# Softmax scores of two head pairs per group, four places for transposed probabilities and an eleven-tile feed-forward in a two-phase attention kernel

## The reference

```python
def _layer(x, wqkv, qs, ksc, wo, lg, lb, w1, b1, w2, b2):
    h = shift_token(x)                       # DIM 256, 8 heads of 64
    q, k, v = jnp.split(h @ wqkv, 3, axis=-1)
    q = l2norm(q) * qs
    k = l2norm(k) * ksc
    q, k = rotary_xpos(q, k)
    o = local_attention(q, k, v)             # windows of 128, each sees itself and the one before
    x = x + o @ wo
    h = shift_token(x)
    h = (h - mu) / jnp.sqrt(var + 1e-05) * lg + lb
    a, g = jnp.split(h @ w1 + b1, 2, axis=-1)    # HID = 682 each
    h = a * jax.nn.gelu(g, approximate=False)
    return x + h @ w2 + b2
```

## Time and profile before

| | |
|---|---|
| median of 3 runs | 5799.47 us (5796.46 to 5799.69) |
| the profiled execution's own time | 5798.98 us |
| its span, first to last instruction | 5797.2 us |
| TensorE busy | 5642.3 us, 97% |
| VectorE, ScalarE, GpSimd busy | 4143.9, 3455.5, 960.7 us |
| mean granted TensorE clock | 0.993 of full speed |

### The profile page before, as it was taken

The page is one execution under the profiler, slowest core; times in us unless marked ns, Lnnn a source line. Parts: engine busy times, 40 slices in busy tenths (PEclk is TensorE's granted clock), DMA queues, the critical chain, the costliest instruction groups (busy, mean ns, idle before and its releaser), DMA issues.

```text
span 5797.2 us, 146068 instructions
## 1 busy us (share of the span) xinstructions
PE 5642.3 (97%) x57904; PEld 2646.8 (46%) x57904; DVE 4143.9 (71%) x10780; ACT 3455.5 (60%) x6979; POOL 960.7 (17%) x1905
## 2 busy tenths in 40 slices
PE   8999999999999999998999999999999999999998
PEld 3444444444444444443444444444444444444443
DVE  6887888788878878786666666666666666666664
ACT  4766666676666667665555555555555555555554
POOL 2222222222222222222000000000000101010100
PEclk9999999999999999999999999999999999999999
DMA  3333333333333333232100000000010000000000
GB/s 70 57 54 67 55 66 56 58 62 51 70 56 65 56 60 60 51 66 52 41 15 8 15 12 12 12 12 15 8 37 12 15 19 15 19 23 12 22 12 19
DMA packets 128424, 215.38 MB, mean 37 GB/s; under 512 B 39964, under 2 KB 40092, under 8 KB 126976
## 3 DMA queue, kind: packets, MB, share of 16 engines
q1 hardware_dynamic: 127744, 206.05, 17.6%
HBM read 45.48 MB, written 25.17 MB: 12 GB/s over the span
## 4 chain that ended last, share of the span: by engine, by line
PE 83%; issue 6%; ACT 6%; DVE 3%; POOL 2%; DMA 0%; POOLq 0%; ACTq 0%; SPq 0%; DVEq 0%
PE ps L564 22%; PE ps L693 14%; PE ps L814 12%; PE ps L996 6%; PE ps L1029 5%; PE ps L890 5%; PE ps L1016 5%; PE ps L898 4%; PE ps L915 4%; ACT pt L1247 3%; PE ps L937 2%; PE ps L866 1%; PE ps L875 1%; PE ps L948 1%; POOL pt L2054 1%
## 5 line engine op out<-in xcount | busy, mean ns | idle before, releaser
L1247 ACT ACTIVATE pt<-ps 128x1024 f32<-128x1024 f32 (+7 forms) x2048 | 1237.3, 653 | 621.4 <-PE ps L564 464.3
L693 PE MATMUL ps<-pt,va 128*32 128x512 f32 (+3 forms) x3072 | 1226.6, 487 | 19.9 <-POOL pt L2054 19.9
L693 PE MATMUL ps<-pt,ones 128*32 128x512 f32 (+3 forms) x6144 | 1236.4, 488 | 0.0
L693 PE MATMUL ps<-pt,vs 128*32 128x512 f32 (+3 forms) x3072 | 1230.1, 488 | 0.0
L1614 DVE CUSTOM_DVE_ANT_0 junk<-ps,causal 128x128 bf16<-128x128 f32 (+3 forms) x2048 | 977.9, 487 | 308.5 <-PE ps L564 292.3
L564 PE MATMUL ps<-kt,qt 96*32 96x512 bf16 (+3 forms) x12288 | 1016.6, 328 | 35.2 <-DVE mc L1614 16.3
L564 PE MATMUL ps<-qt,kt 98*32 98x512 bf16 (+3 forms) x12288 | 835.3, 328 | 22.2 <-ACT pt L1247 21.1
L1618 DVE TENSOR_REDUCE mc<-ps 128x1 f32<-128x512 f32 x1024 | 706.3, 690 | 157.6 <-PE ps L564 127.0
L2054 POOL TENSOR_SCALAR_AFFINE_SELECT pt<-pt 128x256 f32<-128x256 f32 x1024 | 469.5, 459 | 1938.2 <-ACT pt L1247 1936.7
L814 PE MATMUL ps<-wqkv,xs 128*128 128x512 f32 x1536 | 782.3, 619 | 0.0
L1364 ACT ACTIVATE sm<-sm,mxw 128x256 f32<-128x256 f32 (+1 forms) x1024 | 495.7, 485 | 339.4 <-DVE mxw L1783 339.0
(11 more groups left out here) (144 smaller groups left out, 8499.3 us busy)
## 6 DMA issues: line engine op xcount, KB each, us to landing
qt<-part SPq DMA_DIRECT2D x768, 64.0 KB, 2.4
kt<-part SPq DMA_DIRECT2D x768, 64.0 KB, 2.5
ya<-wy SPq DMA_DIRECT2D x128, 128.0 KB, 2.3
yb<-wy SPq DMA_DIRECT2D x128, 128.0 KB, 2.3
xs<-between_phases SPq DMA_DIRECT2D x32, 512.0 KB, 3.9
xt<-in_x SPq DMA_DIRECT2D x16, 512.0 KB, 5.9
between_phases<-z SPq DMA_DIRECT2D x16, 512.0 KB, 2.8
between_phases<-xo SPq DMA_DIRECT2D x16, 512.0 KB, 2.7
```

The source lines that it names most:

```text
L693: mmi = pe.matmul(ps[32 * q:32 * q + 32, 4 + half, lo - half * 512:hi - half * 512], w, probs(kb)[:, i, lo - first(kb):hi - first(kb)], st ...
L1247: act.activation(probs(kb)[:, i, kb * P - first(kb):1024 - first(kb)], ps[:, 2 * i:2 * i + 2, :].rearrange("p a q -> p (a q)")[:, kb * P:1 ...
```

## The change

It does four things.

1. Scores. The two head pairs 0 and 1 are issued one behind the other, and so are 2 and 3. The even pair uses columns 0 to 255 of banks 4 and 5, the odd pair columns 256 to 511. Only the even pair waits for `s_read`, and `largest` of either pair waits until both are made.
2. `ptw` has four places; the copy of pair `hp` waits for `weigh` of the same pair in the window before. In c = 0, 1 and 3 the four `weigh` of a window now stand together; in c = 2 they stand in three pieces.
3. The feed-forward uses tiles of 128 channels: five for the gate, five for the other half, and one of 106 rows of output that holds the last 42 channels of both (42 of the one, then 42 of the other from row 64 on). `hidden` has five tiles instead of six; `gated` of the sixth multiplies two tiles of SBUF, of 42 rows. `ffn_out` keeps 2 x 6 matmuls, the last with 42 rows.
4. The orders of the instructions on TensorE, ScalarE and VectorE are laid anew for each c. Some tiles change their addresses (`pt`, `cn`, `sqf`, `both`), and `fbank` alternates with m, since a half now has an odd number of uses of the two banks.

```diff
-HP = -(-HID // HB)
+HLAST = HID - (HB - 1) * P
+HPAIR = 64 + HLAST
-def fbank(use):
+def fbank(m, use):
-    return 2 if use % 2 else 7
+    return 2 if (m + use) % 2 else 7
+def score_cols(hp, n):
+    return slice(hp % 2 * 256, hp % 2 * 256 + n)
...
-        ptw = sb("ptw", [P, 2, 4, P], F32)
+        ptw = sb("ptw", [P, 4, 4, P], F32)
-        w1 = sb("w1", [P, 2, 2, HB, HP], F32)
-        w2 = sb("w2", [HP, HB, 256], F32)
+        w1 = sb("w1", [P, 2, 2 * HB - 1, P], F32)
+        w2 = sb("w2", [P, HB, 256], F32)
...
-                pe.wait_ge(s_read, done(W * 4 + hp))
+                if hp % 2 == 0:
+                    pe.wait_ge(s_read, done(W * 4 + hp))
                 n = P if W % WIN == 0 else 256
                 for q in range(2):
                     rows = slice(64 * q, 64 * q + 64)
-                    pe.matmul(ps[:, 4 + q, 0:n], qp[rows, hp, :],
+                    pe.matmul(ps[:, 4 + q, score_cols(hp, n)], qp[rows, hp, :],
...
-                    mmi = pe.matmul(ps[0:HP, fbank(6 + j), :], w1[:, kc, 1, j, :], cn[:, kc, :], start=kc == 0, stop=kc == 1)
+                    if j < HB - 1:
+                        mmi = pe.matmul(ps[:, fbank(m, 6 + j), :], w1[:, kc, j, :], cn[:, kc, :], start=kc == 0, stop=kc == 1)
+                    else:
+                        mmi = pe.matmul(ps[0:HPAIR, fbank(m, 6 + j), :], w1[:, kc, 2 * HB - 2, 0:HPAIR], cn[:, kc, :],
+                                        start=kc == 0, stop=kc == 1)
...
-                act.wait_ge(o_full, done(W * 4 + hp - 1))
+                act.wait_ge(o_full, done(W * 4 + hp - 3))
...
-                dve.wait_ge(s_full, done((W * 4 + hp) * 2 + 2))
+                dve.wait_ge(s_full, done((W * 4 + (hp | 1)) * 2 + 2))
...
+                else:
+                    dve.tensor_tensor(hh[0:HLAST, j, :], gb_[0:HLAST, j, :], glast[:, :], ALU.mult).then_inc(hh_done, 1)
```

More of the change, by code:

```diff
@@ L947, in mean @@
                 pe.wait_ge(xsum_done, done(m + 1))
-                pe.matmul(ps[:, fbank(3), :], mean_w[:], both[:, 0, :], start=True, stop=True).then_inc(fm_full, 1)
+                pe.matmul(ps[:, fbank(m, 3), :], mean_w[:], both[:, 0, :], start=True, stop=True).then_inc(fm_full, 1)
             def variance(m):
@@ L955, in variance @@
                 pe.wait_ge(ssum_done, done(m + 1))
-                pe.matmul(ps[:, fbank(4), :], mean_w[:], both[:, 1, :], start=True, stop=True).then_inc(fv_full, 1)
+                pe.matmul(ps[:, fbank(m, 4), :], mean_w[:], both[:, 1, :], start=True, stop=True).then_inc(fv_full, 1)
             def final_mean(m, W):
@@ L1015, in hidden @@
                 for kc in kcs:
-                    mmi = pe.matmul(ps[0:HP, fbank(13 + j), :], w1[:, kc, 0, j, :], cn[:, kc, :], start=kc == 0, stop=kc == 1)
+                    mmi = pe.matmul(ps[:, fbank(m, 13 + j), :], w1[:, kc, HB - 1 + j, :], cn[:, kc, :], start=kc == 0, stop=kc == 1)
                 if kcs[-1] == 1:
@@ L1065, in attend @@
                     scores(W + 1, 0)
+                    scores(W + 1, 1)
                 elif c == 1:
@@ L1073, in attend @@
                     transpose_p(W, 0)
+                    values(W, 0)
+                    final_mean(m - 1, W)
                     scores(W, 2)
+                    scores(W, 3)
+                    transpose_p(W, 1)
+                    values(W, 1)
+                    gate(m, 0, True, (0,))
+                    gate(m, 0, True, (1,))
+                    gate(m, 1, True, (0,))
+                    gate(m, 1, True, (1,))
+                    gate(m, 2, True, (0,))
+                    transpose_p(W, 2)
+                    gate(m, 2, True, (1,))
+                    gate(m, 3, True, (0,))
+                    gate(m, 3, True, (1,))
+                    transpose_p(W, 3)
+                    gate(m, 4, True, (0,))
+                    weigh(W, 0)
+                    weigh(W, 1)
+                    weigh(W, 2)
+                    weigh(W, 3)
+                    transpose_q(W + 1)
+                    gate(m, 4, True, (1,))
+                    gate(m, 5, True, (0,))
+                    transpose_k(W + 1)
+                    gate(m, 5, True, (1,))
+                    scores(W + 1, 0)
+                    scores(W + 1, 1)
+                elif c == 2:
+                    queries(W + 1, 0)
+                    queries(W + 1, 1)
+                    keys(W + 1, 0)
+                    keys(W + 1, 1)
+                    final_variance(m - 1, W)
+                    transpose_p(W, 0)
                     values(W, 0)
@@ L1077, in attend @@
                     transpose_p(W, 1)
-                    final_mean(m - 1, W)
+                    scores(W, 2)
                     scores(W, 3)
[L1080 to L1106, removed]
-                    values(W, 0)
-                    transpose_p(W, 0)
-                    values(W, 1)
-                    final_variance(m - 1, W)
-                    scores(W, 2)
                     hidden(m, 0, True, (0,))
@@ L1175, in _ @@
             scores(0, 0)
+            scores(0, 1)
             for W in range(LAST):
@@ L1186, in _ @@
                 gate(m, j, False)
-            for j in range(HB):
+            for j in range(HB - 1):
                 hidden(m, j, False)
```

230 lines of the change are left out of this document (122 added, 108 removed).

## The result

The changed kernel takes 5648.9 us (median of 4 runs, 5647.3 to 5651.5) against 5799.0 us before: a ratio of 0.974, 95% interval 0.973 to 0.976. The forecast was 5677, with a range from 5642 to 5734. The time fell by 150 us where 122 were forecast.

A forecast was written before the change was run, and what follows sets the result against it. TensorE's list of matmuls was taken to bound the second phase. Savings of 54.9 + 51 + 22 + 22 less 28 us of new waits gave 122 us, so 5799.0 became 5677 us, range 5642 to 5734.

The forecast's parts named there:

- What bounds the kernel: Second phase, 32 periods: as long as TensorE's list of matmuls takes to stream; the first phase costed at nothing.
- Eleven tiles: Feed-forward: each of the 32 halves loses one tile of two matmuls, 54.9 us off TensorE's list, nothing added.
- Scores in groups: Scores on TensorE: 256 fewer groups at 0.19 us each, plus 2.8 us for shared ways in, together 51 us less.
- the two bounds: Time of a group's second pair of scores: 0.43 us or 0.63 + 0.20; the term would be 103 or 0 us.
- `weigh` in larger pieces: Pieces of `weigh` on TensorE fall from 256 to 192, which with what follows them saves 22 us.
- Old and new waits: TensorE: old waits of `mean` and `hidden` go, 22 us less; new waits, mostly in c = 2, add 28 us.
- waits over bank 3: Three places in c = 2 where TensorE waits on transpose and copy: 0.27, 0.27 and 0.08 us a period.
- the third: Wait in c = 2 from `transpose_q` to `transpose_k`, 1.35 us of the 1.43 needed: 0.08 us late.
- Transpose 2 of c = 2: TensorE there waits for ScalarE's copy of pair 1: 16.6 us against 16.5, called level, with 0.05 us allowed.
- the groups do not merge: Rival: the second pair of a group drains the array like a lone one, 49 us lost, 5726 us; chance 0.06.
- The softmax chain: Rival: exponentials and copies behind long blocks bound some windows, 1 to 2 us a period more, 5709 to 5741; chance 0.15.
- The slower case: Rival: ScalarE's lateness at transpose 2 of c = 2 outlasts the period; at 5 us a period 5837 us; chance 0.03.

## Why the prediction was right, and where it was off

*What bounds the kernel* was right: the span followed TensorE's list of matmuls. The first phase did not move; the second phase's first projection starts at 2710.7 us in one trace and 2710.5 in the other.

*Eleven tiles*, 54.9 us: right as a length of the list, and wrong as a cost of nothing added. "The other tiles have 128 channels for 114, and stream the same 512 columns" was looked at for the tiles that grew, and not for the one that shrank to 42 rows: it costs 19 us by the medians and 21 by the profiled spans, shown by the runs with 128, 96, 64 and 42 rows. And in the old order taking the tile away did not pay, as the eleven tiles alone show (9 us slower with 42 rows, 6 us faster with 128). That it pays in the new order is read from the rows; no run has the new order with twelve tiles.

*Scores in groups*, 51 us: this is the mis-sized term. The mechanism was right, the size was near the upper of the two bounds that the text gave, 103. The failed step is the value taken for the second pair: "I take 0.63, because the two passes inside a lone pair already follow one another in the same half array and take 0.315 each". The changed kernel's row shows 0.43. In it only the first pass of a group is slow (0.32 us between the starts of the first two passes of one half, and 0.215 from then on), as the first whole-array matmul after a switch is; the last pass is followed by 0.10 us of way out. The two passes of a lone pair take 0.315 in the mean for two different reasons, 0.32 with the slow start and 0.31 with the way out. I had seen the slow first pass behind a group and not recognised the same thing inside one, where a lone pair has nothing but a first pass and a last. With 0.39 in place of 0.19 the term is about 100 us; the old order with groups gave 76 with its new waits (100 without them), and the new order without groups lost 103 in the list.

*`weigh` in larger pieces*, 22 us: about right. A piece costs 0.30 us (measured by splitting 96 of them), and 64 went: 19 us. By the starts of the two traces it is 27, with what followed them.

*Old and new waits*, 22 gained and 28 lost: right in place, and too low by some 10 us. Two of the waits over bank 3 came where the text put them, at 0.27 (as forecast) and 0.18 (0.27); the third, forecast at 0.08, is 0.04 at most. Two were underrated.

- Transpose 2 of c = 2 waits 0.43 us in the first layer and 0.31 in the second, where 0.05 was forecast. ScalarE kept to the forecast: its copy let the transpose start 16.60 us after the scores of pair 0 (3919.71 to 3936.31), and 16.5 was forecast. TensorE would have been there after 3928.06 - 3919.71 + 7.82 = 16.17 us instead of 16.6, because its two groups of scores took 1.06 us each and not 1.27. So this miss follows from that of the groups: part of what they gained came back as a wait.
- The variance waits for GpSimd, and the forecast allowed 0.22 us a period for it and `mean` together. The rows before, and then after:

```profile
4049.37 1.13 PE L814 MATMUL ps<-wqkv,xs 128*128 128x512 f32 x2
4050.33 1.02 PE L956 MATMUL ps<-both,mean_w 128*128 128x512 f32 x2
```

```profile
3984.04 2.84 PE L821 MATMUL ps<-wqkv,xs 128*128 128x512 f32 x6
3986.93 1.13 PE L964 MATMUL ps<-both,mean_w 128*128 128x512 f32 x2
3987.90 1.02 PE L821 MATMUL ps<-wqkv,xs 128*128 128x512 f32 x2
```

Before, the one matmul behind the scores took 0.96, as it does without a wait. After, the three matmuls take 2.89 us where 2.67 would do, and the variance 0.97 where 0.86 would: 0.33 us a period, 10 us in all, which the list of waits doesn't show, since the weight load does the waiting.

Added up over all starts of the second phase in the two traces, the sum is 54.9 for the tiles, less 22 for the 42 rows (64 x 0.34), 100 for the groups and 30 for `weigh` and for groups that share a way in with it (22 + 3 forecast), less 16 for waits (28 - 22 = 6 forecast): 147 us, against 147.5 between the spans. So the forecast of 122 came as near as it did partly by luck: the groups and `weigh` gave 57 us more than forecast, and the 42 rows and the waits took 32 more. The split between list and waits follows the rule given above, to a few us; it is a closing of accounts, and not a proof of each part.

*The rivals.* That the groups do not merge is excluded by the row of 1.06 us. The softmax chain did not become the bound (TensorE's idle time for ScalarE adds up to 9.3 us in 2550). The slower case did not come either. A kin of it did with the groups taken apart: there VectorE's lateness reached TensorE in every period, and with the dearer list the kernel was 11 us slower than the one before.

## What to carry to other kernels

On an array that several matmuls share, count the switches of form: here a group of scores costs about 0.39 us beyond its streaming, with one pair or with two, and a piece of `weigh` about 0.30, so put as many side by side as PSUM holds (more than two pairs were not tried), and fill a ragged last tile with zero rows until it counts as a whole one (96 were enough). Price a joined group by its bounds, and look for what the first pass after any switch has in common. Read a wait of TensorE from start to start: the idle time in its row was 0.06 to 0.2 us short of what it cost, and the variance's wait stood in no row.

A matmul that one removes may have been the cover of a copy. Look at what stood before and behind it on the path, above all where a single bank is handed back and forth, and move something else there. In a balanced order a shortened wait of 0.25 us need not be worth 0.25 us: here it turned into another engine's wait, in both runs that tried it.

## What the runs showed of the hardware that was not expected

- A matmul with 42 or 64 rows of 128, amid whole ones, costs 0.29 to 0.39 us more, by what follows it; with 96 or 128 rows it costs nothing extra (5648.9 and 5651.4 us against 5627.3 and 5630.2), and directly ahead of scores 42 rows cost nothing (1.81 us against 1.82). The Trainium skill, page "TensorEngine Tiling (Array Packing)", section Available Configurations, names forms of 32, 64 and 128 rows only; the runs fit this, for 42 rows cost what 64 do, and 96 what 128 do. Its rule in the section Key Properties, that a change of form drains the engine, fits the 0.09 us on each way in and out; the trace shows a slow first pass besides.
- In a row of half-array matmuls the weights of the next pass load beside the running one, in the same half of the array: 0.43 us for a pair of 256 columns (3927.00 to 3928.06, less the 0.63 of a lone pair). The two heads of a pair start within 0.01 us of each other; one after the other, by the pace of a pass, they would take 4 x 0.215 = 0.86 us (an estimate). Only the first pass of the group is longer, by about 0.10 us.
- GpSimd's four small steps took 2.3 us beside two operations of VectorE that read both inputs from SBUF, and 1.1 us in the other 96 windows of the same program, beside long ones that read one input from PSUM.
